# Two subtractions of the activation rounding move from GpSimd to VectorE, and a slab's up-branch product moves ahead of the rounding's second half

## The reference

```python
xn = layernorm(x)
# branch 1: gated linear recurrence along the sequence
g, v, d = xn @ Wg + bg, xn @ Wv + bv, xn @ Wd + bd
h = linear_scan(sigmoid(g) * tanh(v), 0.001 + 0.998 * sigmoid(d))
# branch 2: a feed-forward layer with quantized weights and activations
def act_quant(x):                     # per token
    scale = 127.0 / clip(max(abs(x)), 1e-05)
    return clip(round(x * scale), -128.0, 127.0) / scale
gate = silu(act_quant(xn) @ ternary(w_gate).T)       # 1024 -> 4096
up   = act_quant(xn) @ ternary(w_up).T               # 1024 -> 4096
out  = x + h + act_quant(gate * up) @ ternary(w_down).T   # 4096 -> 1024
```

## Time and profile before

| | us |
|---|---|
| median of 2 runs | 7211.08 (7208.06 to 7214.09) |
| the profiled execution's own time | 7208.41 |
| its span, core 2, the slowest | 7206.2 |
| spans of the eight cores | 7132.7 to 7206.2 |
| busy time on core 2 | TensorE 1975.9; VectorE 2787.8; GpSimd 1307.4; ScalarE 395.6 |

### The profile page before, as it was taken

How to read it: one execution, slowest core, us unless ns; L and a number is a source line. 1 busy time by engine, 2 the same in 40 slices (tenths; PEclk the granted TensorE clock), 3 DMA queues, 4 the chain that set the end, 5 groups by cost and what they waited for, 6 DMA issues and landing times.

```text
span 7206.2 us, 45049 instructions; the slowest of 8 cores (7132.7 to 7206.2 us)
## 1 busy us (share of the span) xinstructions
PE 1975.9 (27%) x9367; PEld 976.8 (14%) x9490; DVE 2787.8 (39%) x4389; ACT 395.6 (5%) x676; POOL 1307.4 (18%) x993
## 2 busy tenths in 40 slices
PE   0033333331000000000000045555544454445552
PEld 0022222221000000000000022222222222212220
DVE  2344444445111131113111155555444444455552
ACT  1111111110000000000000000000000000000000
POOL 0000000000111101110111033333333333333331
PEclk9966666665555555555555587777777777777776
DMA  3111111113111131113111413333333333333334
GB/s 88 56 44 41 41 43 49 41 41 112 47 47 47 53 108 47 47 47 125 47 47 47 130 27 94 91 89 93 94 93 92 94 94 92 91 93 95 90 96 128
DMA packets 684076, 529.77 MB, mean 74 GB/s; under 512 B 531184, under 2 KB 531216, under 8 KB 677664
## 3 DMA queue, kind: packets, MB, share of 16 engines
q1 hardware_dynamic: 680192, 520.51, 25.5%
q0 software_dynamic: 3616, 6.38, 0.6%
HBM read 348.21 MB, written 109.05 MB: 63 GB/s over the span
## 4 chain that ended last, share of the span: by engine, by line
SPq 36%; DVE 21%; DMA 17%; PE 11%; issue 7%; POOL 5%; ACT 2%; DVEq 1%; POOLq 0%; ACTq 0%; another core or an unknown queue 0%
SPq L558 13%; SPq L285 11%; SPq L765 4%; POOL pqstage L271 4%; PE pb L793 3%; PE pb L789 3%; SPq L689 2%; DVE qg L511 2%; DMA pbuf<-wdown 2%; PE pb L705 2%; SPq L395 2%; PE pb L443 2%; DVE x_grp L268 2%; DVE x_grp L266 2%; DMA pbuf<-wgate 2%
## 5 line engine op out<-in xcount | busy, mean ns | idle before, releaser
L789 PE MATMUL pb<-wqg,xqF_t 128*128 128x512 bf16 x1968 | 828.9, 421 | 1073.9 <-DMA xqF_t<-scr_xq 1047.2
L793 PE MATMUL pb<-wqu,xqF_t 128*128 128x512 bf16 x2048 | 854.2, 417 | 795.8 <-DMA xqF_t<-scr_xq 789.8
L271 POOL TENSOR_TENSOR pqstage<-x_grp 128x512 bf16<-128x512 f32 x192 | 264.9, 1380 | 3780.8 <-DVE x_grp L268 3780.8
L443 PE MATMUL pb<-wqu,wqg 128*128 128x256 bf16 x3072 | 390.1, 289 | 1123.3 <-DMA wqu<-scr_xn 1123.3
L264 DVE TENSOR_SCALAR qt<-pbuf,wsc 128x512 f32<-128x512 f32 x192 | 94.4, 492 | 1553.5 <-DMA pbuf<-wdown 524.9
L705 PE MATMUL pb<-wdr,pqs 128*128 128x512 bf16 x2005 | 541.9, 400 | 417.9 <-DMA pqs<-scr_pqF 406.8
L257 POOL TENSOR_TENSOR x_grp<-x_grp 128x512 f32<-128x512 f32 x256 | 378.7, 1479 | 1184.9 <-DVE x_grp L254 1184.9
L820 DVE SCALAR_TENSOR_TENSOR pbuf<-pb,dvecs,epi 128x512 f32<-128x512 f32 x256 | 192.2, 751 | 871.6 <-ACT epi L803 853.9
L789 PEld LDWEIGHTS pb<-wqg,xqF_t 128*128 128x128 bf16 x2048 | 219.4, 107 | 2180.2 <-issue 1990.3
L443 PEld LDWEIGHTS pb<-wqu,wqg 128*128 128x128 bf16 x3072 | 311.6, 104 | 1178.9 <-issue 1126.7
L483 PE MATMUL pb<-scal,ones_sb 128*1 128x1 f32 x6 | 0.6, 163 | 1675.1 <-DVE scal L514 1675.1
(11 more groups left out here) (85 smaller groups left out, 2216.2 us busy)
## 6 DMA issues: line engine op xcount, KB each, us to landing
wdr<-scr_wdT SPq DMA_DIRECT2D x512, 256.0 KB, 3.0
pbuf<-wdown SPq DMA_DIRECT2D x64, 512.0 KB, 4.3
pbuf<-wgate SPq DMA_DIRECT2D x64, 512.0 KB, 3.8
pbuf<-wup SPq DMA_DIRECT2D x64, 512.0 KB, 3.9
scr_pqF<-pqstage SPq DMA_DIRECT2D x32, 1024.0 KB, 4.4
pqs<-scr_pqF SPq DMA_DIRECT2D x1024, 32.0 KB, 2.6
pbuf<-x SPq DMA_DIRECT2D x32, 512.0 KB, 3.3
x_grp<-x SPq DMA_DIRECT2D x32, 512.0 KB, 4.9
```

The costliest lines, as they stand in the source:

```text
L271: e.tensor_tensor(o, a, b, OP.subtract), wait=(vb,))
L443: e.matmul(o, l, r, start=st, stop=sp),
L789: e.matmul(o, l, r, start=st, stop=sp),
L793: e.matmul(o, l, r, start=st, stop=sp),
```

## The change

- The two subtractions of `b1_tail` are issued on VectorE in place of GpSimd, so that a piece's rounding ends with a VectorE operation, and SP's transposes wait for VectorE in place of GpSimd.
- In a slab the order on VectorE becomes: front of piece s, product of slab s (line 810 in the new numbering), tail of piece s - 1. Before it was tail, front, product.
- The scaled piece has two buffers in turn (`qt` and an unused part of `x_grp[1]`), and the front waits for the GpSimd difference of two pieces ago where it waited for that of the piece before.
- The wait for the roll buffer's earlier transposes moves from the front of a piece to its tail.

```diff
+        qtP = [qt[:, 0:512], x_grp[1][:, 1024:1536]]
+
         def gq_front(src_ap, s_vec_ap, par, qt_guard=(), pre_wait=()):
             cmP = gcm[par]
+            tP = qtP[par]
             ndX = qnd[:, 0:512] if par == 0 else gnd2
-            op("v", lambda e, a=src_ap, sv=s_vec_ap, o=qt[:, 0:512]:
+            op("v", lambda e, a=src_ap, sv=s_vec_ap, o=tP:
                e.tensor_scalar(o, a, sv, None, OP.mult),
                wait=tuple(pre_wait) + tuple(qt_guard))
-            op("v", lambda e, a=qt[:, 0:512], o=qci[:, 0:512]:
+            op("v", lambda e, a=tP, o=qci[:, 0:512]:
                e.tensor_scalar(o, a, MAGIC, None, OP.add))
...
-            op("gc", lambda e, a=cmP, b=qt[:, 0:512], o=ndX:
+            op("gc", lambda e, a=cmP, b=tP, o=ndX:
                e.tensor_tensor(o, a, b, OP.subtract), wait=(vf,))
...
-            vb = wv(V)
-            op("gc", lambda e, a=gb2, b=gb1, o=gc1:
-               e.tensor_tensor(o, a, b, OP.subtract), wait=(vb,))
-            op("gc", lambda e, a=gc1, b=cmP, o=dst_ap:
+            op("v", lambda e, a=gb2, b=gb1, o=gc1:
                e.tensor_tensor(o, a, b, OP.subtract))
-            return wv(GC)
+            op("v", lambda e, a=gc1, b=cmP, o=dst_ap:
+               e.tensor_tensor(o, a, b, OP.subtract))
+            return wv(V)
...
         def b1_front(ti, pc):
-            pw = []
+            pk = (ti, pc - 2) if (ti, pc - 2) in gqs else (ti - 1, pc + 6)
+            qg = (gqs[pk][2],) if pk in gqs else ()
+            gqs[(ti, pc)] = gq_front(pbuf[:, pc * 512:(pc + 1) * 512],
+                                     scal[:, 1:2], pc % 2, qt_guard=qg)
+
+        def b1_tail(ti, pc):
+            bg = []
             if (ti, pc) in roll_reader:
-                pw.append(roll_reader[(ti, pc)])
...
+                bg.append(roll_reader[(ti, pc)])
+            gfin[(ti, pc)] = gq_tail(gqs[(ti, pc)], roll[pc % 4],
+                                     b_guard=tuple(bg))
...
                 if i > 0:
+                    b1_front(i - 1, s_)
+                op("v", lambda e, i_=pu_, o=pbuf[:, s_ * 512:(s_ + 1) * 512], sc=dvecs[:, 1:2],
+                   sg=sg2[spar]:
+                   e.scalar_tensor_tensor(o, i_, sc, sg, OP.mult, OP.mult),
+                   wait=(silu_mark,))
+                sg2_marks[spar] = wv(V)
+                bank_marks[bku] = wv(V)
+                if i > 0:
                     if s_ >= 1:
                         b1_tail(i - 1, s_ - 1)
                     if s_ >= 3:
...
                         b1_xpose_piece(i - 1, s_ - 3, extra=ex)
-                    b1_front(i - 1, s_)
-                op("v", lambda e, i_=pu_, o=pbuf[:, s_ * 512:(s_ + 1) * 512], sc=dvecs[:, 1:2],
...
```

More of the change, by code:

```diff
@@ L634, in b1_front @@
         def b1_front(ti, pc):
-            pw = []
-            if (ti, pc) in roll_reader:
-                pw.append(roll_reader[(ti, pc)])
[L638 to L647, removed]
+            pk = (ti, pc - 2) if (ti, pc - 2) in gqs else (ti - 1, pc + 6)
[4 more added lines that the diff above has]
+            bg = []
+            if (ti, pc) in roll_reader:
+                bg.append(roll_reader[(ti, pc)])
+            gfin[(ti, pc)] = gq_tail(gqs[(ti, pc)], roll[pc % 4],
+                                     b_guard=tuple(bg))
         def b1_store(ti):
```

## The result

The changed kernel takes 7267.08 us (median of 11 runs, 7243.46 to 7282.47) where the kernel before takes 7212.16 (10 runs): the ratio is 1.0076, with a 95% interval of 1.0064 to 1.0089. It is slower by 55 us. The forecast was +32 us, a median of 7243 in a range of 7200 to 7265.

A forecast was written before the change was run, and what follows sets the result against it. SP's queue was taken as the bound. Piece 0 +34, piece 6 +3, tiles 1 and 2 -7 and the end +2 gave +32 us, a median of 7243 us, in a range of 7200 to 7265.

The forecast's parts named there:

- What bounds the kernel: In the loop, SP's queue sets the pace: 8.05 us per slab against VectorE's 6.60.
- Piece 0: Tiles 3 to 31: its tail behind slab 1's product makes SP's first transpose late, mostly by 1.33 us; 34 us in all.
- Piece 6: End of a tile: its tail behind the last product makes SP wait in five tiles; 3 us in all.
- The addition on VectorE hidden: Tiles 3 to 31: two more VectorE operations per tail cost nothing, the slab taking 5.70 us in place of 6.60.
- Tiles 0 to 2: In tiles 1 and 2, where VectorE sets the pace, shorter slabs gain 7 us, between -12 and -5.
- The end: Last tile and drain: row maximum +4.4 us, drain's last piece -2.4 us; together +2 us.
- The row maximum: In each tile it starts 4.4 us later, but what needs it comes over 20 us after or waits for loads: nothing.
- Rival 1: Piece 0's lateness is made up within the tile by slack in the loads behind it: 7206 us, 12%.
- Rivals 2 and 3: VectorE bounds the slabs after all, 7010 us, 2%; or VectorE becomes the bound in slabs 3 to 7, 7388 us, 3%.
- A change below about 2% is not told apart from none.: For the whole kernel's time: the forecast slowdown of 0.4% lies below what can be told from no change.

The follow-up runs named there:

- e8: The kernel before with the down projection's loads issued on ScalarE, ahead of each slab's silu, in place of SP: 7016.05 us, ratio 0.9727.
- e10: e8 with a tile's activations transposed one tile ahead: 6482.47 us, ratio 0.8986.
- e5: The changed kernel with only piece 0's tail moved back ahead of the product, in slab 1: 7227.17 us, ratio 1.0026.
- e3: The changed kernel with the order front, tail, product in every slab: 7222.92 us, ratio 1.0017.
- e1: The changed kernel with the old order (tail, front, product), so only the subtractions on VectorE: 7224.2 us, ratio 1.0015.
- e11: e9 with a tile's activations transposed one tile ahead: 6486.38 us, ratio 0.8986.
- e0: The changed kernel run once more, unaltered, beside the kernel before: 7264.99 us, ratio 1.0081.
- e6: The kernel before with two empty VectorE operations per slab of tiles 1 to 31, 496 in all: 7219.91 us, ratio 1.0015.
- e15: e6 with four empty VectorE operations per slab in place of two, 992 in all: 7256.01 us, ratio 1.0054.
- e2: The kernel before with only the new order and one more guard, subtractions still on GpSimd: 7321.97 us, ratio 1.0155.
- e9: e5 with the down projection's loads issued on ScalarE, ahead of each slab's silu: 6963.55 us, ratio 0.9658.
- e7: The kernel before with an unused 50 MB scratch tensor ahead of the others in memory and one small copy into it: 7210.44 us, ratio 1.0000.

## Why the prediction was right and wrong

- **What bounds the kernel.** Right. SP's queue: e8 and e10, built on that reading, gave -200 and -734 us where about -210 and -710 to -760 were expected.
- **Piece 0, +34 us.** Right in place and size: 4.97 us from the silu to SP in place of 4.9, and +34.4 us in tiles 3 to 30 between the slowest cores (32.9 over all). e5 shows it alone.
- **Piece 6, +3 us.** Not told apart. From 4380 to 7070 us SP waited for a last operation that wrote into `qtmp`, where pieces 2, 3, 6 and 7 go, once and for 0.4 us on the slowest core, and for 2.9 us in total on average over the eight. e5's tiles 3 to 30 are 3.1 us longer than e3's, a size that two cores of one kernel can differ by.
- **The addition on VectorE hidden, lines 241 and 243 at 0.43.** Right; e1's loop is no longer than the one before.
- **Tiles 0 to 2, -7 us.** Measured -5.9. A slab takes 6.07 us in tile 1, with the conflict of two SBUF inputs, where 6.1 was taken; tile 1's store comes 3.3 us earlier after the first silu (87.7 against 91.0) where 3.8 was forecast.
- **The end, +2 us.** Measured +4.7 between the two slowest cores, and +0.5 for the time behind the last silu on average over all.
- **The row maximum, 4.4 us later, nothing.** Right in this kernel. e11 shows what it costs where nothing hides it.
- **Rivals.** Rival 1 (hidden) fell: the tiles grew by what SP waited. Rivals 2 and 3 fell: VectorE neither was nor became the bound.
- **"A change below about 2% is not told apart from none."** Wrong. The interval of the ratio, 1.0064 to 1.0089, lies wholly above 1.
- **The step that failed is the sum.** It had no term for the stretch ahead of the loop, on no ground but that the code there is unchanged: "34 + 3 - 7 + 2 = +32 us". In the profiled executions the loop and its end grew by 33 us between the slowest cores, as forecast, and 27 us stand ahead of the loop (13 on average over the cores, 24 in e0). By the medians it is 55 against 32, so 23 us are missing. e6 and e15 show that 496 and 992 empty VectorE operations cost 0.15% (11 us) and 0.54% with no work. So about half of the 23 us goes with the length of VectorE's program, by medians whose interval is wide (2 to 19 us for e6); how that length acts on the stretch, and where the other half comes from, stays open. The direction was right, and so was the forecast that the change stays within 2%; the time lay 2 us above the range.

## What to carry to other kernels

Where one queue issues all DMAs in order, look in its timeline for the first command of a tile that has no slack ahead of it. A producer that becomes 1.4 us late there costs that much in every tile, even if the engine that produces has time to spare everywhere else; in the changed kernel the late tails of the other pieces cost 4 us of the loop at most. A longer delay reaches them too: in e2 SP waited for piece 6 as well. Moving work to a busier engine can be free and moving it later can be dear, so price the two apart. And before trimming instructions from an engine that waits for a queue, relieve the queue: here that was worth 10%, while the change, with piece 0 put ahead, brought about 0.7% beside a partly relieved queue (e9 against e8) and nothing beside a fully relieved one (e11 against e10). There the next place without slack was the row maximum, and the order made that late too.

## What the runs showed that was not expected

- With a longer VectorE program, loads issued by SP were slower in the first 290 us, while the empty ones that were added run only from 4177 us on: 512 KB of `x` landed in 3.3, 3.5 and 3.6 us (medians of 32 on core 2) with 0, 496 and 992 empty VectorE operations more. With 496 on GpSimd it stayed at 3.3.
- e1, e3 and e6 do different things and have the same ratio, 1.0015 to 1.0017. A few tenths of a per cent that a change "costs" can lie outside the code that it touches; a kernel with empty instructions is the control for it. A stretch of one profiled execution is not: in e7, with a ratio of 1.0000, the one ahead of the loop was 12 us longer too.
- VectorE's addition over 128x512 takes 0.43 us alone and 1.30 beside a GpSimd subtraction, so that after the change eight operations per slab keep VectorE busy for no longer than six did (2780.7 against 2787.8 us).
